# A selective-scan block on one core of Trainium2: the next batch's first normalisation moved into the third and fourth sequence, and all batch stages on new steps

## What is computed

```python
def _gn(v, G=32): ...            # group norm: 8 channels x 1024 positions share a mean and a variance
def block_a(x, words):           # nearest of 256 words by cosine, per position
    sim = einsum('bchw,nc->bnhw', x / norm(x, 1), words / norm(words, 1))
    near = words[argmin((1 - sim) / 2)]
    return where(min((1 - sim) / 2) < 0.625, near, x)
def block_b(x):                  # layer norm, four Mamba sequences of 64 channels, layer norm, projection
    xn = layer_norm(x)           # over the 256 channels, per position
    for q in range(4):           # chunk q: 64 channels, 128 inner channels, 16 states, 1024 steps
        xc = silu(conv4(in_proj(xn_q))); z = silu(in_z(xn_q))
        B, C, dt = x_proj(xc); dt = softplus(dt_proj(dt) + bias)
        h[t] = exp(dt[t] * A) * h[t-1] + dt[t] * xc[t] * B[t]
        y[t] = sum_states(h[t] * C[t]) + D * xc[t]
        out_q = out_proj(y * z) + skip * xn_q
    return proj(layer_norm(out)) + b
x = x + block_a(_gn(x)); x = x + block_b(_gn(x))
```

## Time and profile before

| | |
|---|---|
| median of 3 runs | 4431.17 us |
| the profiled execution | 4433.55 us |
| its span, first to last instruction | 4431.7 us |
| VectorE busy | 4003.7 us, 90% |
| TensorE busy (matmuls) | 3779.5 us, 85% |
| GpSimd busy | 3427.9 us, 77% |
| ScalarE busy | 2810.5 us, 63% |
| mean granted clock of TensorE | 0.932 of 2.4 GHz |
| DMA queue of the program | 748.91 MB, 65.7% of 16 engines |

### The profile page before, as it was taken

One profiled execution on the slowest core, in us unless ns is written; L12 is line 12 of the kernel. 1 busy time (PEld: TensorE's weight loads), 2 busy tenths in 40 slices (PEclk: granted clock), 3 DMA queues, 4 the chain that ended last, 5 costly groups with the idle time before them and its releaser, 6 DMA issues. The chain is left out here.

```text
span 4431.7 us, 44302 instructions
## 1 busy us (share of the span) xinstructions
PE 3779.5 (85%) x13840; PEld 1269.6 (29%) x13840; DVE 4003.7 (90%) x3073; ACT 2810.5 (63%) x3528; POOL 3427.9 (77%) x2086
## 2 busy tenths in 40 slices
PE   3688988988888898888989888888988988888896
PEld 2222323223232232323223232232323323232221
DVE  2589899998989999899999989999899998989996
ACT  2566666666666666666666666666666666666653
POOL 2487787787878878888778788787788778788775
PEclk8898998999989999998999989999998999989997
DMA  1657576675757758576675767757576675767763
GB/s 39 154 143 193 149 189 177 174 192 152 190 157 188 201 135 202 148 192 180 167 197 143 200 159 186 201 140 202 140 196 183 164 197 144 198 162 186 193 166 109
DMA packets 217723, 751.74 MB, mean 170 GB/s; under 512 B 27400, under 2 KB 28816, under 8 KB 213392
## 3 DMA queue, kind: packets, MB, share of 16 engines
q1 hardware_dynamic: 217488, 748.91, 65.7%
...
## 5 line engine op out<-in xcount | busy, mean ns | idle before, releaser
L592 POOL TENSOR_TENSOR state<-state,c_all 128x1024 f32<-128x1024 f32 x1024 | 2400.1, 2362 | 252.0 <-DVE state L953 229.5
L953 DVE TENSOR_TENSOR_SCAN state<-dtb,ub 128x1024 f32<-128x1024 f32 x1024 | 2341.0, 2286 | 42.7 <-ACT dtb L795 6.1
L1182 PE MATMUL ub<-u,spr 64*128 64x512 f32 x4096 | 1271.5, 683 | 352.1 <-DVE state L953 349.6
L795 ACT ACTIVATE dtb<-dtb,a_neg 128x1024 f32<-128x1024 f32 x1024 | 1159.7, 1141 | 389.4 <-DMA dtb<-dt_scratch 379.8
L944 DVE TENSOR_TENSOR ub<-ub,b_all 128x1024 f32<-128x1024 f32 x1024 | 1243.1, 1214 | 105.0 <-PE ub L1182 98.8
L1182 PEld LDWEIGHTS ub<-u,spr 64*128 64x128 f32 x4096 | 347.8, 196 | 1160.2 <-DVE state L953 679.6
L1198 PE MATMUL yp<-state,gat 128*32 128x512 f32 x4096 | 583.0, 643 | 6.1 <-POOL state L592 6.1
L1047 PE MATMUL mb<-xs,wtap 128*128 128x512 f32 x512 | 261.4, 657 | 20.1 <-DMA xs<-xn 10.6
L668 ACT ACTIVATE dt<-mb 128x512 f32<-128x512 f32 x128 | 75.8, 592 | 241.7 <-PE mb L1078 241.7
L643 ACT ACTIVATE e_x<-mb,ncb 128x512 f32<-128x512 f32 x128 | 88.0, 687 | 219.1 <-PE mb L1047 219.1
L1061 PE MATMUL mb<-xc,wdt 128*128 128x512 f32 x256 | 153.1, 683 | 78.3 <-ACT ym L715 55.4
(11 more groups left out here) (143 smaller groups left out, 4821.6 us busy)
## 6 DMA issues: line engine op xcount, KB each, us to landing
dtb<-dt_scratch SPq DMA_DIRECT2D x1024, 512.0 KB, 4.8
xs<-xn SPq DMA_DIRECT2D x128, 256.0 KB, 5.3
b_all<-bc_scratch SPq DMA_DIRECT2D x64, 512.0 KB, 6.4
c_all<-bc_scratch SPq DMA_DIRECT2D x64, 512.0 KB, 7.9
xt<-in_x SPq DMA_DIRECT2D x16, 1024.0 KB, 6.6
x_scratch<-xt SPq DMA_DIRECT2D x16, 1024.0 KB, 7.0
...
dt_scratch<-dt SPq DMA_DIRECT2D x128, 128.0 KB, 3.6
```

What stands on the lines that cost most here:

```text
L592: pool.tensor_tensor(v, v, c_all[:, c % 2, :], ALU.mult).then_inc(gated, 1)
L795: act.activation(dtb[:, k, :], dtb[:, k, :], ACT.Exp, scale=a_neg[:, GROUP[g]:GROUP[g] + 1]).then_inc(decayed, 1)
L953: dve.tensor_tensor_scan(state[:, g % STATES, :], dtb[:, k, :], ub[:, g % 2, :], 0.0, ALU.mult, ALU.add).then_inc(scanned, 1)
L1182: last = pe.matmul(ub[:, g % 2, h * HALF:(h + 1) * HALF], spr[lo:lo + TURN, GROUP[g] % 8, :], u[lo:lo + TURN, c % 2, h * HALF:(h + 1) * HA ...
```

## The change

The first group norm of a batch's input, from x_in to a_affine01 (the new tuple EARLY), is taken out of sequence 0 of the batch before and put into sequences 2 and 3 of the batch before that one: at sequence 3 these pieces work for batch b + 2, x_in (sequence 2) too. Those for batch 1 come in a new stretch "pre" at the end of the prologue; batch NB - 2 gets a kind of its own, PENULT, that leaves them out. The tables of all engines get new steps. `Banks` counts the uses through once for every batch, since the order isn't the same in all any more. Two waits for x2_back go (in a_affine0 and c_sq). Work and its counts stay as they are.

```diff
-PE_SEQ = {5: ["prep_xc0", "prep_xc1"], 13: ["prep_raw0"], 14: ["prep_raw1"], 17: ["prep_bc"], 19: ["prep_part0"],
-          20: ["prep_dt0"], 22: ["prep_part1", "prep_dt1"], 24: ["own_z"]}
-ACT_SEQ = {7: ["prep_xc0", "prep_xc1"], 8: ["prep_sig_x"], 15: ["prep_raw0"], 16: ["prep_raw1"],
-           17: ["prep_dt_exp", "prep_dt_one"], 18: ["prep_dt_ln", "prep_bc0"], 19: ["prep_bc1"], 21: ["prep_dt0"],
-           25: ["prep_dt1"], 26: ["own_z0"], 27: ["own_z1", "own_sig_z"]}
-DVE_SEQ = {9: ["post_gate"], 24: ["prep_u0"], 25: ["prep_u1"]}
-POOL_SEQ = {3: ["prep_clamp_x"], 5: ["prep_silu_x"], 16: ["prep_dd"], 24: ["own_clamp_z"], 31: ["own_silu_z"]}
-SP_SEQ = {19: ["prep_bc_store"], 22: ["prep_bc_load"], 23: ["prep_store"]}
...
+PE_SEQ = {5: ["prep_xc0", "prep_xc1"], 13: ["prep_raw0", "prep_raw1"], 15: ["prep_bc"], 19: ["prep_part0"],
+          20: ["prep_dt0"], 21: ["prep_part1"], 22: ["prep_dt1"], 24: ["own_z"]}
+ACT_SEQ = {6: ["prep_xc0", "prep_xc1"], 10: ["prep_sig_x"], 14: ["post_take0", "post_take1"], 15: ["prep_raw0"],
+           16: ["prep_raw1", "prep_dt_exp", "prep_dt_one"], 17: ["prep_bc0", "prep_dt_ln"], 18: ["prep_bc1"],
+           21: ["prep_dt0"], 24: ["prep_dt1"], 26: ["own_z0", "own_z1", "own_sig_z"]}
+DVE_SEQ = {9: ["post_gate"], 23: ["prep_u0"], 25: ["prep_u1"]}
+POOL_SEQ = {1: ["prep_clamp_x"], 6: ["prep_silu_x"], 16: ["prep_dd"], 22: ["own_clamp_z"], 26: ["own_silu_z"]}
+SP_SEQ = {17: ["prep_bc_store"], 22: ["prep_store"], 24: ["prep_bc_load"]}
+PE_BATCH = {(0, 1): ["a_norm0"], (0, 3): ["a_norm1"], (0, 8): ["a_sim00"], (0, 9): ["a_sim01"],
+            (0, 10): ["a_sim10"], (0, 11): ["a_sim11"], (0, 12): ["post_out"],
+            (0, 26): ["a_sim20", "a_sim21", "a_sim30"], (0, 28): ["a_sim31"], (0, 31): ["c_mean0", "c_square0"],
+            (1, 0): ["c_mean1"], (1, 1): ["a_turn0"], (1, 2): ["c_square1"], (1, 6): ["a_keep0"],
+            (1, 7): ["a_turn1"], (1, 8): ["a_word01"], (1, 9): ["a_word00"], (1, 10): ["a_keep1"],
+            (1, 11): ["a_word10", "a_word11", "post_out"], (1, 27): ["c_proj00", "a_group1", "c_proj01"],
+            (1, 29): ["c_proj10", "c_proj11"], (2, 0): ["a_mean0"], (2, 2): ["a_square0"], (2, 6): ["a_mean1"],
+            (2, 8): ["a_square1"], (2, 11): ["post_out"], (3, 7): ["a_group0"], (3, 10): ["post_out"]}
+ACT_BATCH = {(0, 2): ["a_rn"], (0, 8): ["a_near0"], (0, 10): ["a_near1"], (0, 18): ["c_sq0"], (0, 23): ["c_sq1"],
+             (0, 26): ["a_near2"], (0, 28): ["a_near3"], (1, 0): ["c_msq0"], (1, 2): ["c_rs0"], (1, 4): ["c_msq1"],
+             (1, 5): ["a_oht0"], (1, 6): ["a_oht1"], (1, 11): ["c_rs1"], (1, 18): ["a_sum10"], (1, 22): ["a_sum11"],
+             (2, 0): ["a_rstd1"], (2, 1): ["a_affine10", "a_affine11"], (2, 2): ["a_msq0"], (2, 8): ["a_rs0"],
+             (2, 12): ["a_msq1"], (2, 13): ["a_rs1"], (2, 22): ["a_xn0", "a_xn1"], (3, 2): ["a_sum00"],
+             (3, 4): ["a_sum01"], (3, 11): ["a_rstd0"], (3, 20): ["a_affine00", "a_affine01"]}
+DVE_BATCH = {(0, 9): ["a_pick0"], (0, 20): ["a_pick1"], (0, 29): ["a_pick2"], (1, 1): ["c_var0", "c_ctr0"],
+             (1, 2): ["a_pick3"], (1, 4): ["c_var1", "c_ctr1"], (1, 7): ["a_keep0"], (1, 9): ["a_mix00"],
+             (1, 11): ["a_mix01", "a_keep1"], (1, 12): ["a_mix10", "a_mix11"], (1, 28): ["a_gm1", "c_out00"],
+             (1, 29): ["c_out01"], (1, 31): ["c_out10", "c_out11"], (2, 5): ["a_var0", "a_ctr0"],
+             (2, 11): ["a_var1", "a_ctr1"], (3, 9): ["a_gm0"]}
+POOL_BATCH = {(0, 5): ["a_xg0", "a_xg1"], (0, 11): ["a_hot0"], (0, 17): ["a_hot1"], (0, 27): ["a_hot2"],
+              (0, 28): ["a_hot3"], (1, 9): ["a_x20"], (1, 12): ["a_x21", "c_scale0"], (1, 16): ["c_scale1"],
+              (1, 23): ["a_mom1"], (1, 24): ["a_newton1"], (2, 3): ["a_scale0"], (2, 14): ["a_scale1"],
+              (3, 3): ["a_mom0", "a_newton0"]}
+SP_BATCH = {(0, 14): ["xs3"], (0, 15): ["x2_back"], (1, 28): ["out"], (2, 7): ["x2_store"], (2, 8): ["out_wait"],
+            (2, 23): ["xs0"], (2, 28): ["x_in"], (3, 9): ["xs1"], (3, 10): ["xs2"]}
+EARLY = ("x_in", "a_sum00", "a_sum01", "a_group0", "a_gm0", "a_mom0", "a_rstd0", "a_newton0", "a_affine00",
+         "a_affine01")
...
+        if kind == PENULT and name in EARLY:
+            continue
...
-                    await_(a_sqd[1], NJ * t)
-                    await_(s_x2st, 16 * t)
-                    sp.dma_start(xt[:], x_v[t]).then_inc(s_x, 16)
+                    await_(a_sqd[1], NJ * (b + 2))
+                    await_(s_x2st, 16 * (b + 2))
+                    sp.dma_start(xt[:], x_v[b + 2]).then_inc(s_x, 16)
...
-                t = b + 1
+                t = b + 2 if c == NC - 1 and name in EARLY else b + 1
...
-                        at_least(act, s_x2ld, 16 * b)
...
-                    act.wait_ge(s_x2ld, 16 * b)
...
+            for name in ("a_sum00", "a_sum01", "a_rstd0", "a_affine00", "a_affine01"):
+                do(name, "pre", -1, NC - 1)
             decay(0, 0, 0)
```

More of the change, by code:

```diff
@@ L74 @@
-DVE_BATCH = {(0, 12): ["a_gm0"], (0, 31): ["a_pick0", "a_pick1"], (1, 1): ["a_pick2", "a_pick3"],
[4 rows of a table removed]
[L79 to L84, removed]
@@ L87 @@
-FIRST, LOOP, LAST = "first", "loop", "last"
+PE_SEQ = {5: ["prep_xc0", "prep_xc1"], 13: ["prep_raw0", "prep_raw1"], 15: ["prep_bc"], 19: ["prep_part0"],
[3 more added lines that the diff above has]
+           21: ["prep_dt0"], 24: ["prep_dt1"], 26: ["own_z0", "own_z1", "own_sig_z"]}
@@ L90, in plan, with kind_of @@
+EARLY = ("x_in", "a_sum00", "a_sum01", "a_group0", "a_gm0", "a_mom0", "a_rstd0", "a_newton0", "a_affine00",
+         "a_affine01")
+FIRST, LOOP, PENULT, LAST = "first", "loop", "penultimate", "last"
+def kind_of(b):
+    return {0: FIRST, NB - 2: PENULT, NB - 1: LAST}.get(b, LOOP)
 def plan(seq_plan, batch_plan, kind, c, j):
@@ L146, in __init__, with note @@
     def __init__(self):
-        self.at, self.count = {}, {}
+        self.at, self.used = {}, [0, 0]
         self.note("pro", SETUP_USES + [u for n in A_ALL for u in bank_use(n, 0)]
                   + [u for n in PREP_ALL for u in bank_use(n, NC - 1)])
-        for kind in (FIRST, LOOP, LAST):
-            self.note(kind, [u for c in range(NC) for j in range(SEQ_STEPS)
-                             for n in plan(PE_SEQ, PE_BATCH, kind, c, j) for u in bank_use(n, c)])
+        self.note("pre", bank_use("a_group0", 0))
+        for b in range(NB):
+            self.note(b, [u for c in range(NC) for j in range(SEQ_STEPS)
+                          for n in plan(PE_SEQ, PE_BATCH, kind_of(b), c, j) for u in bank_use(n, c)])
         self.note("tail", [u for n in ["post_out"] + C_STATS + C_PROJ for u in bank_use(n, 0)])
-    def note(self, kind, uses):
-        n = [0, 0]
+    def note(self, turn, uses):
         for bank, key in uses:
-            self.at[kind, key] = (bank, n[bank])
-            n[bank] += 1
-        self.count[kind] = n
+            self.used[bank] += 1
+            self.at[turn, key] = (bank, self.used[bank])
     def __call__(self, kind, b, key):
[L164 to L176, removed]
+        return self.at[kind if kind in ("pro", "pre", "tail") else b, key]
 def build(nc, x, words, cols, w_in, w_z, w_taps, w_bc, w_dt, w_xdt, w_out, w_proj,
@@ L476, in _ @@
                 load_chunk(c, 0, "pro", -1)
+            do("x_in", "pre", -1)
             store_bc(0, 0)
@@ L481, in _ @@
                 load_unit(0, 0, g)
[L482 to L485, removed]
+            for b in range(NB):
+                turn(kind_of(b), b)
             do("x2_back", "tail", NB)
@@ L609, in _ @@
                 do(name, "pro", -1, NC - 1)
[L610 to L613, removed]
+            for name in ("a_mom0", "a_newton0"):
+                do(name, "pre", -1, NC - 1)
+            for b in range(NB):
+                turn(kind_of(b), b)
             do("c_scale0", "tail", NB, 0)
@@ L827, in _ @@
                 do(name, "pro", -1, NC - 1)
+            for name in ("a_sum00", "a_sum01", "a_rstd0", "a_affine00", "a_affine01"):
+                do(name, "pre", -1, NC - 1)
             decay(0, 0, 0)
-            turn(FIRST, 0)
-            for b in range(1, NB - 1):
-                turn(LOOP, b)
-            turn(LAST, NB - 1)
+            for b in range(NB):
+                turn(kind_of(b), b)
             for name in ("post_take0", "post_take1", "c_sq0", "c_sq1", "c_msq0", "c_rs0", "c_msq1", "c_rs1"):
@@ L1016, in _ @@
                 do(name, "pro", -1, NC - 1)
-            turn(FIRST, 0)
-            for b in range(1, NB - 1):
-                turn(LOOP, b)
-            turn(LAST, NB - 1)
+            do("a_gm0", "pre", -1, NC - 1)
+            for b in range(NB):
+                turn(kind_of(b), b)
             for name in ("post_gate", "c_var0", "c_ctr0", "c_var1", "c_ctr1", "c_out00", "c_out01", "c_out10", "c_out11"):
@@ L1168, in do, with sequence_ready @@
                     last.then_inc(m_full[bank], 1)
-            def sequence_ready(kind, b, c):
+            def sequence_ready(turn_of, c):
```

(11 more changed lines are left out.)

5 lines of the change are left out of this document (1 added, 4 removed), and 17 rows, old and new, of tables (ACT_BATCH, DVE_BATCH, PE_BATCH).

## The result

The changed kernel takes 4614.09 us (median of 4, 4604.57 to 4623.34) against 4431.99 beside it: ratio 1.041, 95% interval 1.039 to 1.043. It is slower by 182 us; 4327 was forecast, in a range of 4262 to 4410. The profiled execution took 4623.34 us, its span 4621.5. One execution of one experiment (8745 us, in a slow state) is left out of its median.

The account below looks back on a forecast made before the run. VectorE, nearly full, bounds the kernel; of 14.2 us of waits a batch 6.8 stay, gaining 7.4 over 15 batches (111), less 6 at the start: 105 off 4433.55 gives 4328.5, median 2.4 lower, 4327 us; range 4262 to 4410.

Parts of the forecast that it names:

- SyncE: SyncE's queue: out's later place delays a dtb load, 0.5 us a batch; prep_bc_load behind prep_store costs VectorE nothing.
- The slower rival: Sequences 2 and 3: ScalarE late for a_rstd0 and a_rstd1, GpSimd standing; two units late at both gives 4533; chance 0.12.
- VectorE's work doesn't change: VectorE's own work is the same before and after, so the span falls by just the waits that go.
- the picks: Sequence 0 into 1: similarities and picks spread over separate units; 0.5 of 3.8 us a batch left.
- the waits behind post_take and post_out: Unit 6 and sequence 1: waits of 2.4 and 2.2 us and their like go; 1.0 of 6.0 a batch left.
- the statistics: New steps but the same hand-overs between two banks; variance wait from 1.6 to 1.4 us a batch.
- The first hold: GpSimd, sequence 3: a_mom0 and a_newton0 behind unit 1's gate delay the spread; price 0.8 us a batch.
- the norms at the start of sequence 0: TensorE, steps 1 and 3 of sequence 0: arrears at the low clock, partly slack; 0.8 us a batch.
- The second hold: GpSimd, a_newton1 at step 24 of sequence 1, a_rstd1 at sequence 2's start: ends early enough, 0 us.
- The start: Batch 1's first normalisation goes ahead of ScalarE's first decay, which starts at 161.9 in place of 155.8: +6 us once.

Follow-up runs that it names:

- the last kernel: Changed kernel with SyncE's steps put back, a_mom0, a_newton0 and a_rstd0 later, norms in sequence 3, a_rstd1 and affines earlier: 4324.1 us (0.975).
- the 193: Changed kernel with SyncE's steps put back (4399.9 us), then only prep_bc_store 17, prep_store 22, prep_bc_load 24 as in the change: 193 us.
- the groups: Changed kernel with SyncE's steps put back (4399.9 us), then each group of the changed SyncE steps alone: together 331 us, all at once 214.

## Why the prediction was wrong

*The step that failed* is "SyncE". It put 0.5 us a batch on out and "nothing at VectorE" on prep_bc_load: "the loads of units 0 and 1 share the queue with its 1 MB, at worst 1.5 us of 4". They land 3 to 5 us later, unit 0's in 9.4 to 9.6 us in place of 4.6 to 5.2, and most of those of units 2 and 3 are late too. For x_in it asked only whether the 1 MB comes in time, not what it does to the dtb loads behind it: by itself it costs 45 us. And it never followed prep_bc_store to step 17 or xs2 to (3, 10), where SyncE waits for ScalarE with dtb loads behind, though it had done just that for out and for GpSimd's holds. SyncE's part is 26.1 - 11.8 = 14.3 us a batch. out, the one step that I priced, costs nothing (-1.6 us in all).

*The slower rival* named the form, "ScalarE is late for the holds", and its sign. Its cause, ScalarE's own load, was wrong: that load came out as it had it (43.9 us in sequence 3, "about 45"), and ScalarE is late because its data are. It also left out that late decays stop VectorE with no hold between, 4.3 us at (3, 0) and (0, 0). The evidence that I held against it was misread. I wrote that ScalarE waits for dtb in most units; the earlier trace rows have 175 waits in 12 x 64 = 768 units. In the trace 120 of them are at units 0 to 4 of sequences 0 and 3, where a decay starts as soon as its load has landed, and there the decay of unit 0 ends 2.9 us ahead of its scan, on average over batches 2 to 13. That was the whole reserve. The load came 5 us later, and 0.1 is left. The chance of 0.12 for slower was too small for a change that reorders the queue on which every unit depends.

*Right:* VectorE's work doesn't change; the picks (0.5 left, forecast 0.5); the waits behind post_take and post_out went; the statistics (1.5 at (2, 4), forecast 1.4 for the variance). The first hold was priced at 0.8; once SyncE was put back it showed 0.8 at (3, 8-9). In the changed kernel it was 4.5.

*Mis-sized:* the norms at the start of sequence 0, 0.8 forecast; at (0, 3-5) the kernel with SyncE put back has 3.9, of which 0.5 is the pick, so 3.4, and 0.2 is left when they are moved away. By the rule of the Trainium skill (TensorE: Matmul & The Clock Gate, HAM oscillation) that the prediction named, norms in the thin units would lift the clock. The runs don't bear it out here: at units 1, 2 and 3 of sequence 0 the mean granted clock is 0.55, 0.64 and 0.54 in the changed kernel, 0.67, 0.85 and 0.58 with SyncE put back, and 0.85, 0.91 and 1.00 with the norms (and the first hold) moved as well. The second hold with a_rstd1 was put at 0 and made 2.3 at (2, 2) with SyncE put back. The start: +6 forecast; the first scan comes at 159.65 in place of 157.06. The chain was nearly right (13.2 us from the end of the dt copies at 145.25 to the decay at 158.42, 14.3 forecast), but the prologue before it ended 2.4 us earlier, which I didn't look into.

With SyncE's term right the forecast would have been too low still: 11.8 us are left a batch instead of 6.8, and 4399.9 was measured. The norms are 2.6 of these 5.0, the second hold 2.3, all small ones 0.6, less the 0.5 that out didn't cost. That the last kernel comes out at 4324, near the forecast 4327, is after three more repairs and no credit to it.

Two of the prediction's sums are a little off besides. 2 us left a batch would be 4254, so the range from 4262 begins at 2.5; and the slower rival with one unit late at both holds gives 4430, not 4432. Neither matters to the outcome.

What stays open: how the 53 us of prep_bc_store at 17 and the rest of the 193 divide into queue time and landing time, and, but for the case of (3, 8) and (3, 9), why the groups together cost 117 us less than one by one.
